# A second PSUM bank for the filters' inner layer, taken from the scores, and chains spread over more batches

## The reference, cut to what matters

```python
t = t + attn2(ln(t))      # scores[i,j] = sum_d v[d] * tanh(Wi[i,d] + Wi[j,d]); softmax; times ln(t)
t = t + moe(ln(t))        # 8 experts, the best 2
t = t + linear_attn(ln(t))
t = t + stu(ln(t))        # causal convolution with 16 filters, then a matrix for each filter
```

## Time and profile before

| | us |
|---|---|
| median of 3 runs | 12868.72 (12866.41 to 12869.83) |
| the profiled execution, its own time | 12862.33 |
| its span | 12860.6 |
| of it up to the first token pass | 6196 |
| passes 0 and 1 | 331 and 348 |
| passes 2 to 14, each | 398 to 403 |
| the tail behind pass 15 | 405 |
| PE busy | 11800.5 (92%) |
| VectorE busy | 11390.3 (89%) |
| ScalarE busy | 10907.9 (85%) |

### The profile page before, as it was taken

How to read it: one execution, slowest core, us unless ns; L and a number is a source line. 1 busy time by engine, 2 the same in 40 slices (tenths; PEclk the granted TensorE clock), 3 DMA queues, 4 the chain that set the end, 5 groups by cost and what they waited for, 6 DMA issues and landing times. The chain is left out here.

```text
span 12860.6 us, 298052 instructions
## 1 busy us (share of the span) xinstructions
PE 11800.5 (92%) x123040; PEld 5937.5 (46%) x123040; DVE 11390.3 (89%) x21539; ACT 10907.9 (85%) x7444; POOL 123.5 (1%) x103
## 2 busy tenths in 40 slices
PE   8999999999999999999568989998898988989898
PEld 3333333333333333333234555555555555555556
DVE  9999999999999999999898888888888888888871
ACT  8999999999999999999687877878778787777761
POOL 0000000000000000000000000000000000000000
PEclk9999999999999999999889999999999999999999
DMA  0000000000000000000101111111111111111113
GB/s 14 2 7 2 4 4 2 7 2 7 2 4 4 2 7 2 2 4 2 57 9 29 51 50 46 49 47 52 49 48 48 47 51 49 48 47 49 50 56 96
DMA packets 290040, 355.08 MB, mean 28 GB/s; under 512 B 28040, under 2 KB 242960, under 8 KB 288656
## 3 DMA queue, kind: packets, MB, share of 16 engines
q1 hardware_dynamic: 288656, 335.48, 8.9%
HBM read 314.14 MB, written 21.23 MB: 26 GB/s over the span
## 5 line engine op out<-in xcount | busy, mean ns | idle before, releaser
L276 ACT ACTIVATE c_ring<-c_xn,c_w_neg 128x1568 f32<-128x1568 f32 x3824 | 5791.8, 1604 | 279.6 <-PE c_acc L235 272.7
L235 PE MATMUL c_acc<-c_ring,c_onehot 128*32 128x392 f32 x68608 | 5763.2, 493 | 138.0 <-DVE c_ring L434 77.3
L1107 ACT ACTIVATE t_ring<-t_ring 128x3120 f32<-128x3120 f32 (+56 forms) x2160 | 4501.4, 2111 | 1100.8 <-DVE t_ring L1426 1054.0
L426 DVE TENSOR_SCALAR c_ring<-c_xn,c_w 128x1568 f32<-128x1568 f32 x4752 | 4568.3, 1030 | 93.4 <-PE c_acc L235 93.2
L1426 DVE TENSOR_SCALAR t_ring<-t_proj 128x784 f32<-128x784 f32 (+63 forms) x10240 | 3912.6, 455 | 520.9 <-PE t_psS L1013 495.3
L235 PEld LDWEIGHTS c_acc<-c_ring,c_onehot 128*32 128x32 f32 x68608 | 2217.6, 110 | 3657.5 <-issue 3203.3
L1013 PE MATMUL t_psS<-t_ring,t_vhot 128*32 128x392 f32 (+15 forms) x36864 | 2350.4, 407 | 236.8 <-ACT t_ring L1107 217.4
L970 PE MATMUL t_psC<-t_filter_work 128*128 128x392 f32 (+3 forms) x6144 | 1762.8, 423 | 460.0 <-ACT t_filter_work L1094 459.1
L970 PEld LDWEIGHTS t_psC<-t_filter_work 128*128 128x128 f32 x6144 | 1144.3, 197 | 1340.6 <-ACT t_filter_work L1094 497.6
L1013 PEld LDWEIGHTS t_psS<-t_ring,t_vhot 128*32 128x32 f32 x36864 | 1110.2, 114 | 1249.9 <-issue 410.0
L434 DVE SCALAR_TENSOR_TENSOR c_ring<-c_xn,c_w,c_ring 128x784 f32<-128x784 f32 x1280 | 1264.1, 1029 | 95.9 <-ACT c_ring L276 94.6
(11 more groups left out here) (231 smaller groups left out, 3473.8 us busy)
## 6 DMA issues: line engine op xcount, KB each, us to landing
t_filter_work<-in_toep_dram SPq DMA_DIRECT2D x256, 393.0 KB, 3.4
t_filter_work<-mix_scratch SPq DMA_DIRECT2D x512, 192.0 KB, 2.5
t_filter_work<-in_toep_dram SPq DMA_DIRECT2D x256, 197.0 KB, 3.0
t_filter_work<-mix_scratch SPq DMA_DIRECT2D x512, 64.0 KB, 1.9
mix_scratch<-t_filter_work SPq DMA_DIRECT2D x4, 2048.0 KB, 9.5
c_xin<-in_x_dram SPq DMA_DIRECT2D x8, 784.0 KB, 4.4
x_scratch<-c_x1o SPq DMA_DIRECT2D x8, 784.0 KB, 3.4
t_proj<-x_scratch SPq DMA_DIRECT2D x16, 392.0 KB, 3.4
```

The source lines that it names most:

```text
L235: mm = pe.matmul(acc[32 * g:32 * g + 32, ch, 0:HALF], onehot[:, 31 - r:63 - r], ring[:, s % RING, g, ch * HALF:(ch + 1) * HALF], start=(s ...
L276: ins = act.activation(tile4(ring[:, s % RING, g, :]), window(xn, tap), ACT.Relu, bias=w0_neg[:, tap, 4 * r + g:4 * r + g + 1])
L426: dve.tensor_scalar(tile4(ring[:, s % RING, g, :]), window(xn, tap), w0[:, tap, 4 * r + g:4 * r + g + 1], 0.0, ALU.subtract, ALU.max).then ...
L1107: act.activation(ring[:, st % RINGS, 0:n], ring[:, st % RINGS, 0:n], ACT.Tanh).then_inc(th.s, 1)
```

## The change

1. `psS` shrinks to one buffer of two banks, for all blocks. Blocks 0 to 4 begin at its column 0, block 5 at column 784, the corner at 928. `psZ` gets a bank of its own name, and `psC` gets a second bank: `conv(u)` writes bank u % 2 and waits for the copy-out of `conv(u - 2)`.
2. PE waits at every block's first step for the copy-out of the block just before it; at block 0 for that of block 5 and the corner of the pass before. To bring the copy-outs forward, `AT_EVAC` goes from 1 to -1, which puts them behind the sums of the fourth slot of the next block and not of the sixth.
3. Wide blocks are cut at column 512 and not in the middle: for block 2 that is 512 + 16 columns where it was 264 + 264.
4. The tables move items: blocks 4's and 5's transposes half a batch later; the second and third of q, k, v one batch later each; the linear attention's a steps half a batch to a batch later and its n steps half a batch to a batch later, over three batches where it was two; the last layer norm and `turn_u` one batch later.

```diff
-CORNER_AT = 480
+NARROW_AT = 784; CORNER_AT = 928
@@ width, buffer_of, first_position
-    return wd, n, wd // n
+    return wd, n, min(wd, 512)
-    wd, n, w = width(blk)
-    return 512 - w if n == 2 else 0
+    return NARROW_AT if blk == 5 else 0
@@ tables
-AT_EVAC = 1
+AT_EVAC = -1
...
-         dict(stats=117, aggr=118, norm=120, turn=batch(30, EARLY), evac=123)]
+         dict(stats=120, aggr=121, norm=123, turn=batch(31, EARLY), evac=127)]
...
-AT_LIN = dict(q=batch(22, EARLY), zq=91, eq=92, qout=93, k=batch(22, LATE), zk=92, ek=93, kout=94, v=batch(23, EARLY), vout=95,
+AT_LIN = dict(q=batch(22, EARLY), zq=91, eq=92, qout=93, k=batch(23, EARLY), zk=95, ek=96, kout=97, v=batch(24, EARLY), vout=99,
...
-AT_STU = dict(u=batch(31, EARLY), uev=127, res=batch(3, LATE), ...
+AT_STU = dict(u=batch(32, EARLY), uev=131, res=batch(3, LATE), ...
@@ PSUM
-        psS = pb("psS", [128, 2, 2, 512]); psF = pb("psF", [128, 512]); psC = pb("psC", [128, 512]); psB = pb("psB", [128, 1024])
-        psZ = psS[:, 1, 1, 0:HALF].rearrange("p (a t) -> p a t", a=2)
+        psS = pb("psS", [128, 1024]); psZ_bank = pb("psZ", [128, 512]); psF = pb("psF", [128, 512]); psC = pb("psC", [128, 2, 512]); psB = pb("psB", [128, 1024])
+        psZ = psZ_bank[:, 0:HALF].rearrange("p (a t) -> p a t", a=2)
@@ PE, conv(u)
-                    W(pe, eC, u, d)
-                    out = psC[:, 0:HALF].rearrange("p (f t) -> p f t", f=2)
+                    W(pe, eC, u - 1, d)
+                    out = psC[:, u % 2, 0:HALF].rearrange("p (f t) -> p f t", f=2)
@@ PE, a block's first step
-                        if k == 0: W(pe, Sev, (scored(4) - Sev.k, 0)[pos] if pos < 2 else scored(pos - 2), b)
+                        if k == 0: W(pe, Sev, 0 if pos == 0 else scored(pos - 1), b)
@@ ACT, copy-out of conv(u)
-                    act.activation(UT[:, u % UTS, :], psC[:, 0:HALF], ACT.Copy).then_inc(eC.s, 1)
+                    act.activation(UT[:, u % UTS, :], psC[:, u % 2, 0:HALF], ACT.Copy).then_inc(eC.s, 1)
```

More of the change, by code:

```diff
@@ L551 @@
 AT_LN = [dict(stats=28, aggr=30, norm=32, turn=batch(8, EARLY), evac=35), dict(stats=80, aggr=82, norm=84, turn=batch(21, EARLY), evac=87),
-         dict(stats=117, aggr=118, norm=120, turn=batch(30, EARLY), evac=123)]
+         dict(stats=120, aggr=121, norm=123, turn=batch(31, EARLY), evac=127)]
 AT_MOE = dict(logits=batch(9, EARLY), bias_add=39, exp=40, rank=41, rank2=42, gate=43, turn=batch(11, EARLY), evac=47, bias=batch(12, EARLY), bias_used=51,
               y=[batch(13 + i // 2, (EARLY, LATE)[i % 2]) for i in range(14)], added=[4 * (13 + i // 2) + 3 + i % 2 for i in range(14)])
-AT_LIN = dict(q=batch(22, EARLY), zq=91, eq=92, qout=93, k=batch(22, LATE), zk=92, ek=93, kout=94, v=batch(23, EARLY), vout=95,
-              a=[batch(24 + i // 4, (EARLY, EARLY, LATE, LATE)[i % 4]) for i in (0, 2, 4, 6, 7, 8, 9)], apart=[99, 100, 103, 104, 104, 107, 107],
-              n=[batch(27 + t // 4, (EARLY, EARLY, LATE, LATE)[t % 4]) for t in range(7)], npart=[111, 111, 112, 112, 115, 115, 116])
-AT_STU = dict(u=batch(31, EARLY), uev=127, res=batch(3, LATE), resev=16, conv=[batch(u // 2, (FIRST, SECOND)[u % 2]) for u in range(64)], conved=[4 * (u // 2) + (3, 5)[u % 2] for u in range(64)],
+AT_LIN = dict(q=batch(22, EARLY), zq=91, eq=92, qout=93, k=batch(23, EARLY), zk=95, ek=96, kout=97, v=batch(24, EARLY), vout=99,
+              a=[batch(24, LATE), batch(25, EARLY), batch(25, LATE), batch(26, EARLY), batch(26, EARLY), batch(26, LATE), batch(26, LATE)], apart=[100, 103, 104, 107, 107, 108, 108],
+              n=[batch(27, LATE), batch(27, LATE), batch(28, EARLY), batch(28, EARLY), batch(28, LATE), batch(28, LATE), batch(29, EARLY)], npart=[112, 112, 115, 115, 116, 116, 119])
+AT_STU = dict(u=batch(32, EARLY), uev=131, res=batch(3, LATE), resev=16, conv=[batch(u // 2, (FIRST, SECOND)[u % 2]) for u in range(64)], conved=[4 * (u // 2) + (3, 5)[u % 2] for u in range(64)],
               mix=[batch(1 + m // 2, MIX) for m in range(64)], ar=[batch(1, EARLY), batch(17, EARLY)], out=[68, 1])
@@ L1012, in body @@
                                     c = o + q * wr - first
-                                    ins = pe.matmul(flatS[32 * q:32 * q + 32, at + lo:at + hi], vhot[:, 31 - r:63 - r], ring[:, st % RINGS, c + lo:c + hi],
+                                    ins = pe.matmul(psS[32 * q:32 * q + 32, at + lo:at + hi], vhot[:, 31 - r:63 - r], ring[:, st % RINGS, c + lo:c + hi],
                                                     start=(r == 0), stop=(r == 31), skip_group_check=True)
@@ L1018, in body @@
                     for r in range(TAIL):
-                        ins = pe.matmul(psS[0:32, 1, 0, CORNER_AT:CORNER_AT + TAIL], vhot[:, 31 - r:63 - r], corner[:, TAIL * r:TAIL * (r + 1)], start=(r == 0), stop=(r == TAIL - 1), skip_group_check=True)
+                        ins = pe.matmul(psS[0:32, CORNER_AT:CORNER_AT + TAIL], vhot[:, 31 - r:63 - r], corner[:, TAIL * r:TAIL * (r + 1)], start=(r == 0), stop=(r == TAIL - 1), skip_group_check=True)
                     ins.then_inc(pK.s, 1)
```

21 lines of the change are left out of this document (9 added, 12 removed).

## The result

The changed kernel takes **12498.58 us** (median of 4 runs, 12493.43 to 12504.12) where the one before took 12867.56 (4 runs, 12860.9 to 12869.83). The ratio is 0.9714 with a 95% interval of 0.9697 to 0.9731: 369 us faster, where 246 were forecast. The direction and the main mechanism were right, the size was too small by a third. The time lies inside the range, and 1.4 us beyond the border (12500) at which the prediction's rival begins in which nearly all waits go.

What follows compares the result with a forecast made beforehand. The prediction saw a circle of waits among PE, VectorE and ScalarE in passes 2 to 15, from `psC`'s copy-out behind tanhs. Terms: -44 tail, -221 passes, +19 cut = -246, to 12616 us (12622 on the median's clock); range 12480 to 12800.

Steps and rivals of the forecast that it cites:

- nearly all waits go: Rival: each stretch's smaller idle time is won, 24 us a pass, with tail and 60 from the clock: 12430; chance 0.08.
- tail: After the passes: the second `psC` bank removes PE's 63 waits of 0.68 us between convolutions; gain 44 us.
- stretches of passes 2 to 15: Gain per stretch of a pass, limited by the smaller idle time of PE and VectorE: together 16.8 us a pass.
- start of a pass: PE's first step waits 3.8 us later for block 5's and the corner's copy-outs, mostly absorbed; cost 1 us a pass.
- the cut at 512: Block 2's 16-column matmuls cost at most 0.07 x 32 = 2.4 us a pass, half on the path: 19 us.
- Nothing can be won: Two stretches of a pass, 143 of 400 us, in which PE is busy all the time: no gain there.
- The single score buffer: Inside a pass: at block 1's end PE can come 0.5 us earlier, no more; elsewhere copy-outs end long before PE's batch.
- The clock: TensorE's clock, 0.96 in passes 2 to 15, should rise with fewer waits; counted as nothing, at most 60 us more gain.
- the slower rival: The single score buffer binds at 6 block starts a pass, 3.8 us each, 365 us: about 12990; chance 0.05.
- Waits that only change their names: Rival: in the passes PE then waits before the next step; only 81 us won, to 12788; chance 0.20.
- That the change does nothing: Rival: VectorE's sums set the time to `mixin`, so the passes win nothing: 12850 to 12868; chance 0.05.
- The signs: What would show the forecast right: `psC` waits under 100 us, tanh waits 150 or so, a pass of about 383 us.

Runs made afterwards that it cites:

- experiment 6: Changed kernel, at the pass start: last score copy-outs two sums earlier, 12497.3 us; or 14 unread filler matmuls before PE's first step in passes 3 to 15, 12512.74 us.
- experiment 4: Changed kernel with its wide blocks cut in the middle again: 12498.9 us, ratio 0.9715 to the kernel before.
- experiment 7: Kernel before with the new tables, one `psC` bank, even convolutions copied out one tanh earlier: 12653.42 us; two tanhs earlier: 12854.39 us.
- experiment 2: Kernel before with the five changed tables and nothing else: 12739.31 us, ratio 0.99.
- Experiment 1: Changed kernel, but each convolution waits for the copy-out of the one before again, despite two `psC` banks: 12734.08 us, ratio 0.9898 to the kernel before.
- experiment 5: Changed kernel with the scores' copy-outs one slot later (`AT_EVAC` 0): 12650.31 us; one slot earlier (-2): 12487.71 us.
- experiment 8: Kernel before with unread filler matmuls in front of six convolutions of a pass where PE waits most for `psC`: 12920.82 us, ratio 1.0047.

## Why the prediction was right, and too small

Its sum, term by term:

| term | forecast | shown |
|---|---|---|
| tail | 44 | 54.5: idle time 44.0, PE's busy time 10.5 |
| stretches of passes 2 to 15 | 16.8 x 14 = 235 | at least 312.5, 22.3 a pass with all costs in it |
| start of a pass | -14 | 0 (experiment 6) |
| the cut at 512 | -19 | 0 (experiment 4) |
| stages before pass 2 | 0 | -5 |
| sum on the profiled executions | 246 | 362 |

**What bounds the kernel: right, with one wait missing.** PE in the middle of a batch, VectorE at a full ring, ScalarE without sums: one bank opened it, and experiment 7 shows the cause from its other side, since the same waits shrink when only the copy-out's place is moved. Missing is ScalarE's wait for k, 86.2 us (experiment 2).

**The tail: right, and too small by the waits' other cost.** The idle time fell by the 44.0 forecast. PE's busy time fell too, by 10.5 us over 63 waits, 0.17 us each, with the same 1774 matmuls at the same clock of 1.00. Experiment 1, one wait apart from the change, gives nearly the same: 51.5 us, 10.3 of them busy time. So a wait that breaks a row of matmuls costs more than its idle time. The rows after the change show where it lies: `conv`'s first matmul starts 0.16 us before the end of the row ahead of it (12402.55, against 12401.15 + 1.56), an overlap that a wait takes away. The ends of matmuls are modelled in a profile, so the split between idle and busy is the profile's; the 54.5 us are not.

**The stretches: the term that was too small.** I took some two thirds of the smaller idle time in each, 16.8 of 24 us; 22.3 came. The 24 was added wrongly: by the earlier trace rows the smaller idle time is 2.4 us in the first stretch, not 1.8, and 10.1 in the last, not 7, which makes 27.5. Four things failed in the term. "Nothing can be won" where PE is busy all the time held for the first such stretch (75.6 to 75.2), not for the second (67.1 to 63.4): with the one before it, it won 8.4 of 117.5 us, where I had 5. The last two won 10.9 where I had 9, and 8.3 of them in the one where I had called 6.0 the most: the bound by idle time isn't a bound when busy time shrinks too. There PE's clock rose from 0.82 to 1.00, and the tables took k's three instructions on VectorE out of it (its busy time 22.97 to 20.70). I had looked at the idle time of PE and VectorE, and not at ScalarE's 6.16 us before k's exponential. And the tables, which I had priced only by q's wait, 2 us a pass, are worth 125 us alone (experiment 2). On top of the bank they are worth 33, 2.3 a pass, so that this figure came out right by luck, for a reason that wasn't in the text.

**The single score buffer: right inside a pass, for the slot that was chosen.** At the seam of the earlier trace rows PE now stands 2.75 us, beyond the 2 us that I had named as a sign against the forecast. The sign was a bad one: VectorE bounds that stretch, it kept its 51.4 us, and all such waits together cost 11 us at most (experiment 5, at -2). But the slower rival is real, and one slot away: 152 us. I had passed over the move of `AT_EVAC` from 1 to -1 as one more table entry; at 0 already 152 of the 369 us are gone, and 1 wasn't run.

**The start of a pass: the wait right, its cost wrong.** PE's first step was to come 5.3 us behind the corner's matmuls (8477.2 to 8482.5), 3.8 later than before. In pass 6 it comes 3.69 behind, 2.3 later than the 1.41 of the earlier trace rows, and straight behind the corner's copy-out (8395.71 to 8395.84); the mean of the 12 waits listed is 4.4, the longest 6.5. The 1 us that I charged isn't in the time, nor does an earlier copy-out give any.

**The cut at 512: mis-sized, and hidden.** 0.07 x 32 is 2.2 us a pass and not 2.4. The runs show 0.03 us a step and not 0.07, 16 us of PE's busy time in all, and nothing of it in the time (experiment 4).

**The clock: counted at nothing, and open.** The mean went from 0.96 to 0.98 in passes 2 to 15, which is about 235 us less of time at the lower level of 1.2 GHz (0.04 / 0.5 x 5580 = 446; 0.02 / 0.5 x 5268 = 211), and so by estimate some 118 us less work for PE; 89 us less of busy time were measured. How much of that lies on the path isn't known: all of it in the piece of experiment 8, nothing at the pass start. A kernel that has the waits of the one and the clock of the other in all places wasn't tried.

**The rivals.** Waits that only change their names: 102 us of the new waits are for the score buffer and 60 for tanhs, but 414.6 went. The time it gave, 12788, is not far from what the change gives without its freer wait (12734). Nearly all waits go, at 12430: without the 60 for the clock that would be 12490, and the time came out 9 us above; the chance of 0.08 was too low. It isn't that rival's mechanism, though: PE still waits, and its sum had the wrong 24. That the change does nothing: no. The Trainium skill's "TensorE: Matmul & The Clock Gate", section "HAM oscillation — how this bites in real kernels", tells of a kernel in which PSUM double buffering "gave no further gain"; here the freer wait gives 236 us, and 184.5 of it where ScalarE, which empties the bank, is in order behind its tanhs.

**The signs.** `psC` waits none in the tail (forecast so) and none in the passes (forecast under 100); tanh waits 110.8 (150); VectorE's 480 at 268 ("well down"); PE busy 93.6% (over 93); a pass 376 us (383).

## What to carry to other kernels

Two in-order engines with one buffer between them have to meet at it: the price is what queues behind each of them, not the copy's own half microsecond, and a second buffer or a better slot lowers it (236 and 86 us here). Before adding a buffer, try the slots, one by one, on both sides: one slot moved the time by 11, 86, 152 or 201 us in this kernel. Before adding up gains by the idle time of two engines, list the waits of the third in the same stretch: ScalarE's 86 us before one exponential were the place where the tables gave 112 of their 125 us. And expect the parts of a change to overlap (458 us apart, 366 together).

## What was not expected of the hardware

- A wait cost PE 0.17 us beside its idle time: 63 waits went from the tail with 44.0 us idle and 10.5 us busy.
- Small matmuls in four column groups in turn cost little: a step of block 2 with pieces of 512 and 16 columns has as many matmuls as one cut in the middle, and cost PE 0.03 us more (15.8 us of busy time over 512 steps), nothing in the time. The Trainium skill's "TensorE: Matmul & The Clock Gate", section "Wait — 56ns, not 53.3ns?", would make 0.17 us of them; the earlier trace rows has small matmuls at 13 ns.
- Steps behind 3.7 us of idle time ran at 117 ns a matmul of 512 and fewer columns and a granted clock of 0.75, behind filler at 86 ns and 1.00, and the faster ones won nothing at that place.
